# A two-block convolution network on one core: 3x3 convolutions as 21 matmuls over 128 rows instead of 27 over 96, and the statistics of x on ScalarE

## What is computed

```python
# block 0: four directional depthwise filters of 7 taps, mixed by an attention over
# the directions, then a full 3x3 convolution
feats = [dwconv(gn(x), w) for w in (w_h, w_v, w_d45 * diag, w_d135 * anti)]
context = mean(feats * feats, over points)            # 4*96 numbers
attn = softmax(leaky_relu(context @ w_att1.T) @ w_att2.T, over directions)
x1 = x + conv3x3(sum(attn * feats), w_proj)
# block 1: linear attention plus a DFT branch
q, k, v = conv1x1(gn(x1), w_qkv); q, k = softmax(q), softmax(k)   # over points
out = conv1x1(einsum(k @ v.T, q), w_proj1)
qf = ifft(conv1x1(gelu(conv1x1(fft(gn(x1)).real, w_q1)), w_q2)).real
kf, vf = split(dwconv3x3(conv1x1(out, w_kv), w_kvconv))
y = x1 + conv1x1(softmax(l2norm(qf) @ k.T * temperature) @ vf, w_projf)
```

## Time and profile before

| | |
|---|---|
| median of 3 runs | 3841.41 us (3840.19 to 3842.67) |
| profiled execution, its own time | 3844.74 us |
| its span (first to last instruction) | 3843.1 us |
| mean granted TensorE clock | 0.979 of full speed |
| PE, PEld busy | 3649.9 us (95%), 2998.9 us (78%) |
| DVE, ACT, POOL busy | 3024.8 us (79%), 1642.1 us (43%), 211.1 us (5%) |
| matmuls of the 3x3 convolutions (L970, L971, L976) | 10368 = 16 convolutions x 24 halves x 27 |
| chain that ended last, by engine | PE 56%, DVE 22%, issue 19% |

### The profile page before, as it was taken

One profiled execution on the slowest core, in us unless ns is written; L12 is line 12 of the kernel. 1 busy time (PEld: TensorE's weight loads), 2 busy tenths in 40 slices (PEclk: granted clock), 3 DMA queues, 4 the chain that ended last, 5 costly groups with the idle time before them and its releaser, 6 DMA issues.

```text
span 3843.1 us, 59619 instructions
## 1 busy us (share of the span) xinstructions
PE 3649.9 (95%) x22946; PEld 2998.9 (78%) x22946; DVE 3024.8 (79%) x2829; ACT 1642.1 (43%) x2720; POOL 211.1 (5%) x376
## 2 busy tenths in 40 slices
PE   4659999999999999999999999999999999999998
PEld 2348688968789688886889687896888878897977
DVE  7988998789877898779987898878987798854020
ACT  3422682138521584126821386215841268211630
POOL 1001000100001000010001000010000100010000
PEclk8779999999999999999999999999999999999999
DMA  5355222922147231742229222471317422271002
GB/s 116 98 137 132 66 67 35 225 73 69 48 102 182 59 83 42 167 121 67 66 37 226 71 68 51 110 182 48 87 41 173 112 67 66 39 178 32 1 7 31
DMA packets 164730, 344.35 MB, mean 90 GB/s; under 512 B 110336, under 2 KB 110576, under 8 KB 164432
## 3 DMA queue, kind: packets, MB, share of 16 engines
q1 hardware_dynamic: 141392, 255.36, 27.0%
q0 software_dynamic: 23040, 84.95, 10.0%
HBM read 189.27 MB, written 150.99 MB: 89 GB/s over the span
## 4 chain that ended last, share of the span: by engine, by line
PE 56%; DVE 22%; issue 19%; DMA 1%; ACT 1%; SPq 0%; DVEq 0%; POOL 0%; ACTq 0%; POOLq 0%
DVE feat L715 18%; PE banks L970 11%; PE banks L971 11%; PE banks L976 11%; PE banks L985 6%; PE banks L995 3%; PE banks L1053 3%; PE banks L1015 2%; PE banks L1001 2%; PE banks L1002 2%; PE banks L1039 1%; DMA feat<-feats_d 1%; DVE e_lo L747 1%; DVE e_hi L739 1%; PE banks L1008 0%
## 5 line engine op out<-in xcount | busy, mean ns | idle before, releaser
L715 DVE SCALAR_TENSOR_TENSOR feat<-xin,w,feat 96x1536 f32<-96x1536 f32 x540 | 947.1, 1809 | 1.8
L970 PE MATMUL banks<-e_hi,wp_hi 96*96 96x384 f32 x1728 | 587.4, 340 | 24.3 <-DVE e_lo L848 12.2
L970 PE MATMUL banks<-e_hi,a_hi 96*96 96x384 f32 x1728 | 597.7, 347 | 0.0
L971 PE MATMUL banks<-e_lo,a_hi 96*96 96x384 f32 x1728 | 592.9, 344 | 0.0
L971 PE MATMUL banks<-e_lo,wp_hi 96*96 96x384 f32 x1728 | 586.2, 340 | 0.0
L715 DVE SCALAR_TENSOR_TENSOR feat<-xin,wh,feat 96x1536 f32<-96x1536 f32 x288 | 520.7, 1808 | 28.9 <-ACT feat L497 27.2
L715 DVE SCALAR_TENSOR_TENSOR feat<-xin,wv,feat 96x1536 f32<-96x1536 f32 x288 | 520.8, 1808 | 0.0
L509 ACT ACTIVATE squares<-feat 96x1536 bf16<-96x1536 f32 x192 | 285.2, 1485 | 445.0 <-DVE feat L715 443.0
L976 PE MATMUL banks<-e_hi,a_lo 96*96 96x384 f32 (+1 forms) x1728 | 337.5, 339 | 0.0
L976 PE MATMUL banks<-e_hi,wp_lo 96*96 96x384 f32 (+1 forms) x1728 | 335.7, 338 | 0.0
L575 ACT ACTIVATE res<-banks 96x768 f32<-96x768 f32 x96 | 77.2, 804 | 598.7 <-PE banks L976 598.7
(11 more groups left out here) (152 smaller groups left out, 4854.1 us busy)
## 6 DMA issues: line engine op xcount, KB each, us to landing
feats_d<-feat SPq DMA_DIRECT2D x160, 576.0 KB, 4.1
feat<-feats_d SPq DMA_DIRECT2D x160, 576.0 KB, 6.8
feat<-in_x SPq DMA_DIRECT2D x48, 576.0 KB, 6.9
res<-in_x POOLq DMA_DIRECT2D x96, 288.0 KB, 4.1
out<-x POOLq DMA_DIRECT2D x96, 288.0 KB, 2.8
out<-res POOLq DMA_DIRECT2D x96, 288.0 KB, 4.3
xin<-in_x SPq DMA_DIRECT2D x32, 792.0 KB, 9.0
xin<-in_x SPq DMA_DIRECT2D x16, 684.0 KB, 10.2
```

The costliest lines, as they stand in the source:

```text
L715: dve.scalar_tensor_tensor(out=dst, in0=src, scalar=taps_w[d](k), in1=dst, op0=ALU.mult, op1=ALU.add).then_inc(tap_done, 1)
L970: pe.matmul(dst, whi[:, t, :], rows(e_hi, a0, n, dx), start=(t == CENTRE_FIRST[0]), stop=False)
L971: pe.matmul(dst, whi[:, t, :], rows(e_lo, a0, n, dx), start=False, stop=False)
```

## The change

1. `e_hi` and `e_lo` get 128 partitions. Partitions 96 to 127 of `e_hi` receive channels 0 to 31 of `e_hi` again, those of `e_lo` channels 32 to 63 of `e_hi`. A new buffer `shifted` (96 partitions, two slots) holds channels 64 to 95 of `e_hi` three times, shifted by a row each. So the low weights' products ride along: a half is 9 matmuls of 128 rows over `e_hi` (weight `w1`: high parts, and on the spare rows low parts), 9 over `e_lo` (`w2`), and 3 of 96 rows over `shifted` (`w3`): 21.
2. POOL makes these copies, 5 DMAs of 32 partitions for each group (`fill`), two groups ahead of PE in both convolutions.
3. The weights are prepared with two ACT copies and five DVE subtractions, where there were one and one. PE's attention convolution waits for the first subtraction instead of ACT's copy, with 4 filler matmuls ahead of it (`keep_clock`) instead of 5.
4. The statistics of x: two ACT passes with a running sum (Identity and Square) over each sixth of x, 12 in all at the head of ACT's `start`, replace DVE's 18 `bn_stats`. DVE adds up the 6 partial sums and scales them.
5. `HID_AT` is 10, and the hidden product is at (11, 0), the logits at (11, 1).

```diff
-HID_AT = 7
+HID_AT = 10
-L0_SMALL, L1_SMALL, GN_SMALL = 8, 21, 7
+L0_SMALL, L1_SMALL, GN_SMALL = 8, 25, 7
+SPARE = 32
+SHIFTED = GR * EP + 2
+FILLS = 4
+FILL_DMAS = 5
...
+            def fill(sems, j):
+                lo = 0 if j == 0 else (j * GR + 2) * EP + 1
+                hi = EN if j == NG - 1 else ((j + 1) * GR + 2) * EP + 1
+                done = sems[j % FILLS]
+                pool.dma_start(e_hi[C:C + SPARE, lo:hi], e_hi[0:SPARE, lo:hi]).then_inc(done, 16)
+                pool.dma_start(e_lo[C:C + SPARE, lo:hi], e_hi[SPARE:2 * SPARE, lo:hi]).then_inc(done, 16)
+                for g in range(3):
+                    at = (j * GR + g) * EP
+                    pool.dma_start(shifted[g * SPARE:(g + 1) * SPARE, j % 2, :], e_hi[2 * SPARE:C, at:at + SHIFTED])\
+                        .then_inc(done, 16)
+            def fill_e(i, j):
+                if j < 2:
+                    pool.wait_ge(e_ready, i * U_E + ETILES)
+                else:
+                    pool.wait_ge(fin_ready, i * NG + j - 1)
...
+                pool.wait_ge(e_hi_ready, i * U_E + min(U_E, (j + 1) * GR // TR + 1))
...
+            def fill_fg(b, j, second):
+                if j >= 2:
+                    pool.wait_ge(conv_ready, b * NG + j - 1)
...
+                pool.wait_ge(fg_hi, b * NCH + min(NCH, (j + 1) * GR // CR + 1))
...
+            def x_sums(b):
+                for n in range(NCH):
+                    act.wait_ge(*stat_loaded(b, n))
+                    for k, func in enumerate((ACT.Identity, ACT.Square)):
+                        wait(act, x_stat, 2 * b * NCH + 2 * (n - 1) + k + 1)
+                        act.activation(squares[k][:], feat[:, stat_slot(n)], func, accum_out=xsums[:, k, n:n + 1])\
+                            .then_inc(x_stat, 1)
...
             def start(b):
+                if not first_image(b):
+                    x_sums(b)
                 norm_chunk(b, 0)
...
+            def moments_x(b, st):
+                dve.wait_ge(x_stat, 2 * (b + 1) * NCH)
+                st(dve.tensor_reduce(mv[:], xsums[:], AX.X, ALU.add))
+                st(dve.tensor_scalar(mv[:], mv[:], 1.0 / N, None, ALU.mult))
...
             def start(b, between=lambda: None):
-                for n in range(STATS):
-                    x_stats(b, n, n + 1)
-                    if n % (2 * XSTAT) == 2 * XSTAT - 1 and n + 1 < STATS:
-                        between()
+                between()
+                between()
...
                         for t in CENTRE_FIRST:
                             dst, a0, n, dx = tap(t)
-                            pe.matmul(dst, whi[:, t, :], rows(e_hi, a0, n, dx), start=(t == CENTRE_FIRST[0]), stop=False)
-                            pe.matmul(dst, whi[:, t, :], rows(e_lo, a0, n, dx), start=False, stop=False)
+                            pe.matmul(dst, w1[:, t, :], rows(e_hi, a0, n, dx, 128), start=(t == CENTRE_FIRST[0]), stop=False)
...
                         for t in CENTRE_LAST:
                             dst, a0, n, dx = tap(t)
-                            last = pe.matmul(dst, wlo[:, t, :], rows(e_hi, a0, n, dx), start=False, stop=(t == CENTRE_LAST[-1]))
+                            pe.matmul(dst, w2[:, t, :], rows(e_lo, a0, n, dx, 128), start=False, stop=False)
...
+                        for dx in range(3):
+                            last = pe.matmul(conv_ps[0:C, j % 2, h, 0:TR * W], w3[:, dx, :], shifted_rows(j, h, dx - 1),
+                                             start=False, stop=(dx == 2))
...
-                keep_clock(5, small_ps)
+                keep_clock(4, small_ps)
...
-                    attention_block(b - 1, {(HID_AT, 1): hidden, (HID_AT + 1, 0): logits} if first else {})
+                    attention_block(b - 1, {(HID_AT + 1, 0): hidden, (HID_AT + 1, 1): logits} if first else {})
```

More of the change, by code:

```diff
@@ L243, in build @@
         fin_ready, fin_copied = sem("fin_ready"), sem("fin_copied")
+        fg_filled = [sem(f"fg_filled{n}") for n in range(FILLS)]
+        e_filled = [sem(f"e_filled{n}") for n in range(FILLS)]
         waits_passed = {e.engine: sem(n) for e, n in (
@@ L434, in step @@
                                 .then_inc(res_loaded[j % RES], 16)
+                        if 1 <= j and j + 1 < NG:
+                            fill_fg(b, j + 1, second)
                         if j >= 1:
@@ L508, in square @@
                 wait(act, squared, b * DIRS * NCH + q * DIRS + d)
-                act.activation(squares[0 if first_image(b) else 1][:], feat[:, d], ACT.Square, accum_out=sq[:, d, ch:ch + 1]).then_inc(squared, 1)
+                act.activation(squares[0 if first_image(b) or u <= LEAD else 1][:], feat[:, d], ACT.Square, accum_out=sq[:, d, ch:ch + 1]).then_inc(squared, 1)
             def unit_work(b, u, part=None):
@@ L952, in group_sums, with conv @@
                 pe.matmul(small_ps[0:C, 500:502], group, mv[:], start=True, stop=True).then_inc(done, 1)
-            def conv(i, whi, wlo, done, ready, between={}, low_ready=lambda: None):
+            def conv(w1, w2, w3, done, ready, between={}, second_ready=lambda: None, third_ready=lambda: None):
                 for j in range(NG):
@@ L1141, in ready @@
                             pe.wait_ge(x1_done, b * NG + j - 1)
-                    conv(b, wp_hi, wp_lo, conv_ready, ready, {(GN_AT + 1, 0): lambda: start(b + 1)} if more else {})
+                    conv(wp1, wp2, wp3, conv_ready, ready, {(GN_AT + 1, 0): lambda: start(b + 1)} if more else {})
                     keep_clock(3, stage_ps[:, SLOTS - 1])
```

123 lines of the change are left out of this document (84 added, 39 removed).

## The result

The changed kernel takes 4012.14 us in the median of 4 runs (4008.89 to 4014.61), the kernel before 3841.79. The ratio is 1.0443, with a 95% interval of 1.0425 to 1.0461: slower by 4.4%. The forecast was 3931 us with a range of 3878 to 4020. The sign was right, and the loss, 170 us, is 1.9 times the forecast's. The profiled execution has a span of 4009.3 us, 166 more than before.

What follows compares the result with a forecast made beforehand. It took PE and DVE as closely tied over most of both convolutions, returning features as pacing the products, and DVE's chain the end. Terms summed to +89.7 us on 3844.74, 3934.4; that execution being 3.3 above the median, forecast 3931, range 3878 to 4020.

Steps and rivals of the forecast that it cites:

- behind the products: Last low part to last sum: 7.5 us shorter in images 1 to 6, 4.1 in image 0, 18.3 in image 7.
- late fills: Rival, chance 0.20: fill copies land late and PE goes at their pace; 3963 us, or 4027 if queued behind features.
- products later, seven images: Attention convolution in the loop: products start 24.2 us later in each of seven images.
- products, eight images: Products stretch including fills: 66.9 us, 1.3 shorter in images 1 to 7; 4.0 longer in image 0.
- clock behind it, eight times: PE, done before DVE's last sum, enters norm and maxima at the lower clock: +1.5 us, eight times.
- start: Kernel start: ACT's statistics passes, weight copies and DVE's subtractions make the moments later, +6.3 us.
- step 8: Last attention convolution, running alone with PE setting the pace: 25.5 us shorter.
- The convolutions: A group falls from 54 to 42 matmuls at an unchanged 0.177 us each, 9.56 to 7.43 us.
- The attention convolution in the loop: PE waits for ACT's copies 2, 4 and 6; groups 8 to 10 precede the hidden product; products 24.2 us later.
- The products: Stretch paced by returning features: fills cost 4 us, between bounds 0 and 8.4, giving 66.9 us against 68.20.
- The base of 62.9: Products stretch before adding fills, taken from image 0, without the attention convolution's outputs beside it: 62.9 us.
- From the last low part to the last sum: ACT's moments at +23.4, last sum at +77.5, PE not last: 7.5 us shorter in images 1 to 6.

Runs made afterwards that it cites:

- e2: The changed kernel with only HID_AT set back from 10 to 7, hidden product ahead of group 8: 3899.36 us.
- e3: The changed kernel with ACT taking three copies instead of two ahead of each unit's work: 3871.40 us.
- e9: The changed kernel with every fill DMA in place but cut to 64 elements a partition (8 KB instead of 97): 3927.42 us.
- e1: The changed kernel without the fill copies, the third weight reading e_hi in place of shifted: 3885.51 us.
- e7: The changed kernel with ACT writing the mix convolution's spare partitions, POOL copying only shifted (3 DMAs a group, not 5): 3985.61 us.
- e5: The changed kernel with shifted filled by one DMA of 96 partitions, same bytes but other data: 4003.50 us.
- e4: The kernel before the change, with only the statistics of x moved to ACT: 3844.56 us.
- e11: The changed kernel with 27 matmuls and no fills in the mix convolution, three copies per ACT unit, hidden product between group 10's halves: 3783.39 us.
- e6: The changed kernel with POOL's loads of x rows for x1_sum issued one group earlier: 4027.90 us.

## Why the prediction was half right

What the change does to the attention convolution came out as forecast. Two terms failed, both in the main by the price of the fills: in the products it was taken at half its bound, and behind the products it was left out. They came out 50.8 and 29.7 us too low; the other terms take 5 us of that back. That 4012 lies in the stated range of 3878 to 4020 is luck as far as the forecast goes: its own terms end at 3975, and the range reached further only for the late fills. (From the bounds as stated its lower end comes out at 3887, not 3878; nothing rests on that.)

The terms of the sum over the whole kernel, forecast and measured between the marks:

| term | forecast | measured |
|---|---|---|
| products later, seven images | +169.4 | 6 x 24.1 + 23.0 = +167.6 |
| products, eight images | -5.1 | 6 x 4.8 + 5.8 + 11.1 = +45.7 |
| behind the products | -67.4 | 6 x (-3.2) - 0.5 - 18.0 = -37.7 |
| clock behind it, eight times | +12.0 | 6 x 1.1 + 1.1 + 0.4 = +8.1 |
| start | +6.3 | +6.2 |
| step 8 | -25.5 | -24.3 |
| sum | +89.7 | +165.6 |

The sum of the measured terms is within 1 us of the spans' difference.

- **The convolutions.** Right. ACT copies group 0 of step 8 at 3913.45 and group 11 at 3995.30, 7.44 us a group (forecast 7.43): 128 rows stream as 96 do, at 0.177 us. The two rows:

```profile
3913.45 0.81 ACT L651 ACTIVATE res<-banks 96x768 f32<-96x768 f32 x1 [7.96 <-PE banks L1073]
...
3995.30 0.81 ACT L651 ACTIVATE res<-banks 96x768 f32<-96x768 f32 x1 [6.40 <-PE banks L1073]
```

- **The attention convolution in the loop.** Right in mechanism and size, 24.1 for 24.2 us; e2 and e3 undo it in the two ways that the mechanism allows. The lower clock behind PE's waits for ACT is there.
- **The products.** This step failed in its size. I took 4 us for the fills, the middle of 0 and 8.4. The share of 0.90 in image 0 before was no room: the 8.4 us are what the bytes cost when all of them go (8.2, e9 against the changed kernel), 9.3 with the number (e1). What showed in place of the gaps that I had assumed is DVE waiting for features that come back later, 8.8 us an image more than without fills. The upper bound was the estimate, though e7 says that it is not a plain rate per byte. The base of 62.9 was 1.4 low (e1: 64.3). The prediction's estimate from that page, an upper end of 16.8 us, is about twice what was measured, and by e5 the same bytes through 96 partitions cost nearly as much, so the rule is not where the loss comes from.
- **From the last low part to the last sum.** This step failed for images 0 to 6: right only for image 7 (66.3 for 66, no next x and no norm to wait for). For the others two errors half cancel. I timed ACT's moments at +23.4, and without fills they are at +18.8 (a pass starts 1.47 us after the one before and not 1.70, and the first at +1.1 and not +2.5), so that the stretch would be 73.4 and not 77.5. But I left the fills out of this stretch altogether: I wrote that PE needs its groups from +24 on and is not last. With fills group 5 is late, the group sums behind it too, and that is 8.0 us.
- **The clock behind it.** Right in mechanism, 8.1 us for 12.0. The first 4 us behind the last sum of image 3, before and now (the third column from the end is the clock):

```profile
1721.87:1725.87 4.00, 3.11 (x9) 1.07 (x8) 1.84 (x7) 0.51 (x1) 0.73 (x2) 1.00 0.27 78
```

```profile
1818.73:1822.73 4.00, 2.74 (x5) 1.28 (x6) 1.84 (x7) 0.36 (x1) 0.69 (x2) 0.50 0.27 80
```

  In e4 and e11, where PE is busy up to the last sum, the table's first column stays at 206.8.
- **The rivals.** Late fills stood at 3963 to 4027 with a chance of 0.20. PE does wait for DMA copies in the middle of the mix convolution (240.5 us), which I had named as a sign that I was wrong; 168.6 us of it lie in the products, beside DVE's wait for the features and with no wait of DVE for PE there, and cost nothing by themselves; the 72.5 us behind the products hold those that make group 5 late. PE isn't at the fills' pace in step 8. So that rival's size came true by a mixture: its late fills behind the products, and in the products the features that come back later, which it did not have.
- **The statistics.** On their own they are worth nothing (e4): in the kernel before, PE is the bound in the stretch from which they take DVE's work.

## What to carry to other kernels

When an engine gets faster, list what it waits for at its new pace: here a fixed order on another engine (two copies, then a unit's work) had been free for a slow PE, and taking three copies ahead gave back 141 us. A share of 0.90 on the profile was no room here: the extra copies cost as much as their bytes at the full rate, so the upper bound is the safer estimate, and the place to look is what else those engines bring (here the features). A cheaper convolution that needs copies paid only where the engines had room: 21 matmuls in one convolution and 27 in the other beat both kernels, by 1.5% on the kernel before. Small DMAs cost too when PE waits for each of them and they are issued late: 41.9 us here. Issuing the fills from another queue was not tried.

## What the hardware showed that I had not expected

A fill of 8 KB is not free: with all fills at that size the kernel is still 41.9 us slower than without them, and POOL's busy time is 705.4 us for 225.9. POOL issues a fill every 0.49 us, less than the 0.70 us that I had taken from the earlier trace rows. In image 3 the copies into `shifted` took 6.9 us to land behind the products, 1.9 in the median of the kernel (e9). And loads issued earlier beside busy DMA engines made the kernel slower (e6, 15.8 us) although the wait that they were to remove did go.
